# Values with v as the stationary operand in 32-column strips, sums from products with ones, and no transpose of the heads' output

## What is computed

```python
q = (hidden_states @ Wq.T).reshape(B, S, H, D)        # H = 8 heads of D = 32
k = (hidden_states @ Wk.T).reshape(B, S, H, D)
v = (hidden_states @ Wv.T).reshape(B, S, H, D)
...
q_blocked = ...reshape(B, nb, CHUNK, H, D)            # blocks of CHUNK = 12 queries
k_ctx = _extract_block_context(k, nb)                 # 24 keys for each block
v_ctx = _extract_block_context(v, nb)
matrix_ac = jnp.einsum('bnchd,bnkhd->bhnck', q_blocked, k_ctx)
...
logits = jnp.tanh((matrix_ac + matrix_bd) / SOFTCAP) * SOFTCAP
attn = jax.nn.softmax(logits, axis=-1)
out = jnp.einsum('bhnck,bnkhd->bnchd', attn, v_ctx)
...
return out @ Wpost.T
```

## Time and profile before

| | us |
|---|---|
| median of 3 runs | 770.41 (769.52 to 772.46) |
| the profiled execution | 771.75 |
| its span on the core | 770.0 |
| TensorE busy, share of the span | 97% |
| VectorE | 61% |
| ScalarE | 47% |
| GpSimd | 46% |
| granted TensorE clock, mean | 0.992 of full speed |

### The profile page before, as it was taken

The page is one execution under the profiler, slowest core; times in us unless marked ns, Lnnn a source line. Parts: engine busy times, 40 slices in busy tenths (PEclk is TensorE's granted clock), DMA queues, the critical chain, the costliest instruction groups (busy, mean ns, idle before and its releaser), DMA issues.

```text
span 770.0 us, 19528 instructions
## 1 busy us (share of the span) xinstructions
PE 745.6 (97%) x6487; PEld 688.0 (89%) x6487; DVE 466.4 (61%) x1212; ACT 359.7 (47%) x654; POOL 352.9 (46%) x262
## 2 busy tenths in 40 slices
PE   6999999999999999999999999999999999999993
PEld 5898999999999998899999999999999999999992
DVE  3465368788799975555555555555555555555551
ACT  4667777667666576333333333333333333333330
POOL 3465566666664547133333444434433333344422
PEclk9999999999999999999999999999999999999997
DMA  8543689999998772122473562563463662222221
GB/s 251 155 156 91 186 274 329 313 316 321 307 305 272 199 131 59 40 36 36 100 189 70 143 171 43 129 157 67 108 180 65 154 158 42 41 43 43 40 29 20
DMA packets 66455, 111.07 MB, mean 144 GB/s; under 512 B 15561, under 2 KB 48921, under 8 KB 66361
## 3 DMA queue, kind: packets, MB, share of 16 engines
q0 software_dynamic: 19216, 43.31, 23.7%
q1 hardware_dynamic: 31073, 41.96, 18.8%
q10 hardware_dynamic: 16072, 24.51, 10.0%
HBM read 66.89 MB, written 42.88 MB: 143 GB/s over the span
## 4 chain that ended last, share of the span: by engine, by line
PE 86%; DVE 7%; DMA 3%; issue 2%; ACT 1%; POOL 0%; SPq 0%; ACTq 0%; POOLq 0%; DVEq 0%
PE psum L1417 79%; PE psum L1547 4%; DVE spare_m L1201 3%; DMA bd_d<-arena 1%; PE psum L1505 1%; DMA out<-spare,sca_i 1%; DVE spare_m L1203 1%; PE psum L1432 1%; DVE xg_m L1203 1%; DMA x_all<-in_x 1%; DMA arena<-bd_d 1%; PE psum L1632 1%; PE psum L1623 0%; DVE arena L1353 0%; DVE arena L1297 0%
## 5 line engine op out<-in xcount | busy, mean ns | idle before, releaser
L1417 PE MATMUL psum<-w_ring,xT 128*128 x1206 | 281.1, 379 | 0.5 <-DVE xT L1241 0.5
L1417 PEld LDWEIGHTS psum<-w_ring,xT 128*128 128x128 f32 x1206 | 214.0, 188 | 29.3 <-issue 0.6
L659 POOL DMA_INDIRECT xg<-xn_d,gat_i x67 | 70.2, 1047 | 238.6 <-DVE spare L1403 212.0
L1417 PE MATMUL psum<-w_ring,hT 128*128 x1139 | 152.0, 287 | 1.5 <-DVE spare L1403 1.1
L849 ACT ACTIVATE xT<-psum,nwp 128x128 fp32r<-128x128 f32 x134 | 41.9, 364 | 216.7 <-PE psum L1505 183.1
L1417 PEld LDWEIGHTS psum<-w_ring,hT 128*128 128x128 f32 x1139 | 140.3, 191 | 1.8 <-issue 1.8
L732 POOL DMA_INDIRECT out<-spare,sca_i x67 | 106.7, 1592 | 41.3 <-issue 19.4
L1241 DVE SCALAR_TENSOR_TENSOR xT<-psum,nwp,xT 128x128 fp32r<-128x128 f32 x134 | 40.9, 347 | 135.1 <-ACT xT L849 133.0
L703 POOL TENSOR_TENSOR arena<-arena,const 120x540 f32<-120x540 f32 x38 | 51.0, 1343 | 106.9 <-DVE arena L1287 103.5
L1227 DVE SCALAR_TENSOR_TENSOR spare<-psum,slot_w,spare 128x704 f32<-128x704 f32 x67 | 63.7, 951 | 43.3 <-PE psum L1417 27.0
L1417 PE MATMUL psum<-arena 32*120 32x108 f32 (+1 forms) x1216 | 85.5, 262 | 0.0
(11 more groups left out here) (186 smaller groups left out, 985.4 us busy)
## 6 DMA issues: line engine op xcount, KB each, us to landing
w_split<-w_ring POOLq DMA_DIRECT2D x20, 1088.0 KB, 7.9
w_ring<-w_split SPq DMA_DIRECT2D x40, 544.0 KB
raw<-in_w_raw ACTq DMA_DIRECT2D x20, 544.0 KB, 6.8
w_ring<-in_w_raw ACTq DMA_DIRECT2D x12, 544.0 KB, 5.8
arena<-in_x SPq DMA_DIRECT2D x37, 108.0 KB
out<-arena SPq DMA_DIRECT2D x37, 108.0 KB
arena<-xn_d SPq DMA_DIRECT2D x31, 120.0 KB
x_all<-in_x ACTq DMA_DIRECT2D x2, 1024.0 KB, 7.2
```

The source lines that it names most:

```text
L659: pool.indirect_dma_start(out=xg[:, b % NXG, :], out_offset=None, in_=xn_d, in_offset=bass.IndirectOffsetOnAxis(ap=gat_i[:, b:b + 1], axis=0),
L1417: return pe.matmul(out_ap, lhs, rhs, start=first, stop=last)
```

## The change

`values` is turned round: `v1` loses its column of ones and becomes the stationary operand (120 keys by 32 columns), `ex` the moving one (108 columns). Four heads stand in the four strips of 32 columns of the array and write to the four groups of 32 partitions, so the features are in the partitions from the start. A second set of eight matmuls with a block of ones as the stationary operand gives the sums, repeated over the 32 partitions of each head, in the same layout beside it in bank 6. `divided` now takes the reciprocal of all those sums (128 partitions by 216) into `rden`, and two products write the quotients over the sums in PSUM, one for the odd blocks and one for the even ones, which puts the queries back in order. `turn_out`, `perm_out` and `o_sb` are gone, and `split_out` reads the 108 queries of each half from where the products were written. Its first 12 columns (`PAST`) are zeroed once at the start instead of `o_sb`.

```diff
-        turns = sb("turns", [P, P + 2 * GK], F32R)
+        turns = sb("turns", [P, P + GK], F32R)
...
-        perm_out = turns[0:GK, P + GK:P + 2 * GK]
...
+        rden = at["o"].rearrange("p (k n) -> p k n", k=KD)
...
+        o_ps = psum[:, 6, 0:KD * GQ].rearrange("p (k n) -> p k n", k=KD)
+        o_sums = psum[:, 6, KD * GQ:2 * KD * GQ].rearrange("p (k n) -> p k n", k=KD)
+
+        def by_block(rows):
+
+            return rows.rearrange("p k (n c) -> p k n c", c=CHUNK)
...
-            pool.memset(v1[:, :, :, DH:HV], 1.0).then_inc(s_ini, 1)
-            pool.memset(o_sb[:, :, :], 0.0).then_inc(s_ini, 1)
+            pool.memset(oT_hi[:, :, 0:PAST].bitcast(F32), 0.0).then_inc(s_ini, 1)
+            pool.memset(oT_lo[:, :, 0:PAST].bitcast(F32), 0.0).then_inc(s_ini, 1)
...
             def divided(g):
 
                 dve.wait_ge(s_pv, g + 1)
-                pv = psum[0:GQ, 6, 0:H * HV].rearrange("p (h n) -> p h n", h=H)
-                dve.reciprocal(rden[0:GQ, :], pv[:, :, DH:HV].rearrange("p h n -> p (h n)")).then_inc(s_rc, 1)
+                dve.reciprocal(rden[:, :, :], o_sums).then_inc(s_rc, 1)
                 dve.wait_ge(s_rc, g + 1)
-                if g:
-                    dve.wait_ge(s_ot, g)
-                dve.tensor_tensor(o_sb[0:GQ, :, :], pv[:, :, 0:DH],
-                                  rden[0:GQ, :].rearrange("p (h n) -> p h n", n=1).to_broadcast([GQ, H, DH]),
-                                  ALU.mult).then_inc(s_o, 1)
+                for blocks, first in ((slice(0, NODD), 1), (slice(NODD, GB), 0)):
+                    dve.tensor_tensor(by_block(o_sums)[:, :, first::2, :], by_block(o_ps)[:, :, blocks, :],
+                                      by_block(rden)[:, :, blocks, :], ALU.mult).then_inc(s_o, 1)
...
             def split_out(g):
 
-                dve.wait_ge(s_ot, g + 1)
+                dve.wait_ge(s_o, 2 * (g + 1))
                 if g:
                     dve.wait_ge(s_po, g)
-                o_ps = psum[:, 6, 0:KD * GK].rearrange("p (k n) -> p k n", k=KD)
-                dve.tensor_copy(oT_hi[:, :, :], o_ps).then_inc(s_oth, 1)
+                dve.tensor_copy(oT_hi[:, :, PAST:GK], o_sums).then_inc(s_oth, 1)
                 dve.wait_ge(s_oth, g + 1)
-                dve.tensor_tensor(oT_lo[:, :, :], o_ps, oT_hi[:, :, :].bitcast(F32), ALU.subtract).then_inc(s_ote, 1)
+                dve.tensor_tensor(oT_lo[:, :, PAST:GK], o_sums, oT_hi[:, :, PAST:GK].bitcast(F32),
+                                  ALU.subtract).then_inc(s_ote, 1)
...
             def values(g):
...
-                for h in (*range(HM, H), *range(HM)):
-                    if h == 0:
-                        pe.wait_ge(s_mk, g + 1)
-                    head = HC * (h % KD) + h // KD
-                    ins = mm(psum[0:GQ, 6, head * HV:(head + 1) * HV], ex[0:GK, g % 2, h, :], v1[0:GK, g % 5, head, :],
-                             True, True)
+                pe.wait_ge(s_mk, g + 1)
+
+                for k in range(KD):
+                    for i in range(HC):
+                        r = slice(DH * i, DH * (i + 1))
+                        mm(psum[r, 6, k * GQ:(k + 1) * GQ], v1[0:GK, g % 5, HC * k + i, :], ex[0:GK, g % 2, KD * i + k, :],
+                           True, True)
+                for k in range(KD):
+                    for i in range(HC):
+                        r = slice(DH * i, DH * (i + 1))
+                        ins = mm(psum[r, 6, (KD + k) * GQ:(KD + k + 1) * GQ], ones[0:GK, 0:DH],
+                                 ex[0:GK, g % 2, KD * i + k, :], True, True)
                 ins.then_inc(s_pv, 1)
...
-            def turn_out(g):
-
-                pe.wait_ge(s_o, g + 1)
-                for k in range(KD):
-                    ins = pe.matmul(moved(psum[:, 6, k * GK:(k + 1) * GK]),
-                                    o_m[0:GK, HC * k:HC * (k + 1), :].rearrange("p h n -> p (h n)"), perm_out,
-                                    start=True, stop=True, is_transpose=True)
-                ins.then_inc(s_ot, 1)
...
                 queries(s)
-                if s >= 4:
-                    turn_out(s - 4)
                 keys(s)
```

22 lines of the change are left out of this document (5 added, 17 removed).

## The result

The changed kernel takes 799.17 us (median of 4 runs, 798.22 to 799.71) where the kernel before takes 769.96 us on the same chip (769.15 to 772.46): a ratio of 1.037, with a 95% interval of 1.035 to 1.040. It is slower by 29 us. The prediction had the sign and 787 us; the time lies 2 us above its range of 779 to 797. The profiled execution took 798.77 us, its span 797.0, so 27.0 us more than the span before.

A forecast was written before the change was run, and what follows sets the result against it. TensorE was taken to bound the kernel (97% busy), VectorE the table steps. Plain +5.5, tables +10.4, two steps -0.9, logits +0.5, last groups +1 made +16.5 us: 788.3 profiled, 787 us median, range 779 to 797.

The forecast's parts named there:

- TensorE's gain: On TensorE, `values` falls from 1.54 to 0.94 us and `turn_out`'s 0.19 us goes: 0.79 us less a plain step.
- The reciprocal: On VectorE, 216 elements at 6.2 ns each take 1,490 ns, +1.29 us for each of 38 groups.
- The rival with 8 ns an element: On VectorE, a dearer reciprocal adds 1.6 us of work a group, total 795 us; chance 0.08.
- The products: On VectorE, two products into PSUM take 0.18 + 0.20 us, +0.04; a halved rate would add 0.22 a group.
- Logits steps: Seven steps before 104.48 us: `turn_rows` starts 0.87 us later against 0.79 saved, +0.5 us, within 3 either way.
- Table steps: Eight steps, 215.57 to 278.40 us, paced by VectorE: seven go from 7.83 to 9.11 us, +10.4 in all.
- The 16 plain steps: 104.48 to 215.57 us: five steps at 6.76 us, eleven at 7.5 on average, 116.6 instead of 111.1, +5.5.
- they stay off the path: ScalarE and GpSimd, with 24.12 and 22.46 us of work in five steps of 34.49 us, do not set the time.
- The step that I had at 7.9 us: Plain step 188.03 to 194.92, 6.46 us of VectorE work in 6.89, where VectorE sets the time: becomes 7.9 us.
- The step that I had at 6.76: A free step: TensorE waits 0.67 us for VectorE's split, 3.92 + 2.84 = 6.76 us instead of 6.88.
- The last two steps of the loop: 278.40 to 292.72 us: 13.5 us instead of 14.3 as short waits vanish, -0.9.
- The last groups: 292.72 to 324 us: a chain through the long reciprocal, some 0.3 us longer in three rounds, +1 us.

The follow-up runs named there:

- e1: Changed kernel with the reciprocal over only 8 of 216 columns, the other columns multiplied by ones: 759.6 us, 0.985 of the kernel before.
- e3: Changed kernel with unused matmuls filling TensorE's wait ahead of `project` in every step from 11 on: 798.1 us, 1.032 of the kernel before.
- h4_after_set: Changed kernel; GpSimd subtracts 64 of 1088 weight columns, then fills the other 1024 twice with zeros: 773.4 us, 1.003 of the kernel before.
- h3: Kernel before; GpSimd subtracts 64 of 1088 weight columns, then fills the other 1024 twice with zeros: 769.1 us, ratio 0.997.
- f5: Changed kernel with unused matmuls ahead of `project` only in steps where TensorE waits long: 800.2 us, 1.039 of the kernel before.
- moved versions: Kernels with GpSimd's subtraction put behind `values`: 807.6 us changed, 833.9 before; changed, with raw pieces loaded a step later, 793.6, 790.0 and 787.6.
- h1: Kernel before with GpSimd's weight subtraction cut to 64 of 1088 columns, nothing filled in: 790.9 us, ratio 1.030.
- f1: Changed kernel with one more wait on GpSimd, putting its weight subtraction behind `values`, beside VectorE's reciprocal: 807.6 us, 1.048 of the kernel before.
- f3: Kernel before with one more wait on GpSimd, putting its weight subtraction behind `values`: 833.9 us, ratio 1.082.

## Why the prediction was right in sign and too small

- **TensorE's gain: right.** `values` takes 0.87 us, my lower bound, with 0.94 predicted, and `turn_out` is gone. e1 shows the gain of 0.7 us in each logits step.
- **The reciprocal: right.** 1,502 ns against 1,490. The rival with 8 ns an element gave 795 us, near what came, but it is refuted by the row; its time was near for another reason. The estimate of 1.8 us that I drew from the repeat count of 8 in the Trainium skill (VectorE: DVE Perf Modes, the 8-slice pipeline) falls with it: 6.24 ns an element measured, 8.3 estimated.
- **The products: right.** 266 and 281 ns, the two 0.45 us together; writing PSUM in runs of twelve is not slower.
- **Logits steps: right.** +0.5 predicted, -0.2 measured.
- **Table steps: right in kind.** Two take 9.12 and 9.13 us, 9.11 predicted, and with the waits filled (e3) six of the eight do. The eight took +13.5 us instead of +10.4; the rest is in the first one (12.09 us) and in uneven ones, and with the waits filled it is +10.8, so most of the excess goes with the falls of the clock. The reason that I gave, VectorE without a pause, was only half of it: 3.05 us (mean of eight) of each of those steps was one comparison that takes 1.22 us when it is not held, as these rows of before and of h4_after_set say. My own rows had the sign: the earlier trace rows shows it with 3.15 us for 1024 elements, where I wrote that everything else on VectorE runs at about 1 ns an element.

```profile
L1201 DVE TENSOR_TENSOR spare_m<-const,small 128x1024 fp32r<-128x1024 f32 x8 | 24.4, 3048 | 0.0
```

```profile
L1207 DVE TENSOR_TENSOR spare_m<-const,small 128x1024 fp32r<-128x1024 f32 x8 | 9.7, 1216 | 0.0
```

- **The 16 plain steps: wrong.** +5.5 us predicted, +11.7 measured. The step that failed is "they stay off the path", said of ScalarE and GpSimd from their busy time alone, together with VectorE's average of 5.73 us a step, which I took as a property of its own work. It contained held instructions of up to 1.83 us, which need 0.41 or less; their end is set by GpSimd's, and GpSimd's start is set by VectorE. With the hold cut down, these steps take 111.6 us against 111.1 (h4, h3), so nearly all of the +11.7 goes with it, my +5.5 included. The step that I had at 7.9 us, the heaviest, became 8.20, and five more came to 8.0 to 8.3; a sixth had 9.46, of which 1.2 us go with a fall of the clock (8.22 in f5). The step that I had at 6.76, without routing work, came to 6.74: the path from the reciprocal to `project` was right. My sum itself is off by 0.3 us: five steps at 6.76 and eleven at 7.5 make 116.3, not 116.6.
- **The last two steps of the loop:** -0.9 predicted, +0.1 measured, by the same cause or by the fuller queue ahead of them; not separated.
- **The last groups: mis-sized.** +1 predicted, +4.8 measured. With the hold cut down it is still +2.8 (h3 against h4), so about 2 us of it go with the hold. The other 1.8 us above my term I put down to the chain through the long reciprocal in the three last rounds. It is the reciprocal's length in some way: with 8 and 108 columns this stretch takes 33.1 and 35.2 us, with 216 39.4. How much of it is the granted clock, which falls twice for 3.4 us here, once in h4 and never in the kernel before, no run takes apart.
- **ScalarE's exponentials** (`turn`, L1478, 0.24 us a step in the rows above) are a new short wait that I had not named; it lies inside the time that TensorE has to spare.

The sum by stretches, predicted and measured: logits +0.5 and -0.2, plain +5.5 and +11.7, tables +10.4 and +13.5, two steps -0.9 and +0.1, last groups +1 and +4.8, experts 0 and +0.2, start 0 and -3.0 (within its own scatter); +16.5 and +27.1.

What the runs don't settle is what the first table step and the seam at step 35 pay in the moved versions, and where in the last groups the +2.8 us stand. That the kernel before gains so little from the shorter hold (62.8 to 61.6 us in the table steps, nothing in the plain ones) is no riddle: in h3_before_set TensorE is busy for all of both stretches, as its row for the table steps says (61.61 of 61.61 us), with 48.82 us of VectorE beside it.

```profile
214.02:275.63 61.61, 61.61 (x755) 60.42 (x754) 48.82 (x142) 39.80 (x74) 29.74 (x35) 1.00 0.85 240
```

## What to carry to other kernels

Before work is given to an engine with "room", look at its longest instructions of a short form: where one form has two very different durations, and the long one ends with an instruction of another engine, the time is a hold and not work, and it will move with the change. An engine is off the path only if nothing that it releases, or holds, comes back to the engine that sets the time; follow one turn of that loop in the timeline and add the new work to it, rather than to a sum of busy times. To take a suspected hold away in an experiment, keep the end of the other engine's work and the transfer behind it as they are, or they can hide the answer, as in h1; and look whether the hold is gone or has only moved to another instruction, as in f1 and f3.
